# All casts of a LayerNorm on one engine, and the input loaded in eight transfers instead of two

## The chip, the cores and the metric

The kernel runs on all 8 cores of one Trainium2 chip. Each core computes one of the 8 sequences of the batch on its own; the cores exchange nothing. The metric is the device time of the slowest core in microseconds (us).

## The reference, cut to what matters

x has the shape (8, 2048, 1024): per core 2048 tokens of 1024 features. One layer is computed, a feed-forward block, an attention block with its own MLP, and the same feed-forward block again:

```python
x = x + 0.5 * ffn(layernorm(x), W_r, W_k, W_v, mu_r, mu_k)
x = x + attn(layernorm(x), ...)      # two more LayerNorms inside: ln1 ahead of the attention, ln2 ahead of the MLP
x = x + 0.5 * ffn(layernorm(x), W_r, W_k, W_v, mu_r, mu_k)

def layernorm(x, eps=1e-5):
    m = mean(x); v = var(x)
    return (x - m) / sqrt(v + eps)

def ffn(x, ...):
    x_prev = x shifted by one token
    xr = mu_r * x + (1 - mu_r) * x_prev ; xk = mu_k * x + (1 - mu_k) * x_prev
    return sigmoid(xr @ W_r.T) * (square(relu(xk @ W_k.T)) @ W_v.T)
```

The statistics of ln1 are worked out from those of the LayerNorm ahead of it, so the kernel measures mean and variance four times: ahead of the first feed-forward block, ahead of the attention, ahead of the MLP, and ahead of the second feed-forward block.

## The kernel before, in words

The data lie with features on the partitions: 8 chunks (`CH`) of 128 features, each with 2048 tokens (`T`) in its row. `S` is the f32 buffer [128, 8 x 2048] with x; chunk c stands in the columns T*c to T*(c+1). In the DRAM tensor `x_in` the layout is the same.

Work is put into one list for each engine by a small class: `p.t` is TensorE (PE), `p.v` VectorE (DVE), `p.s` ScalarE (ACT), `p.y` DMAs issued by SyncE (SP), `p.g` DMAs issued by GpSimd (POOL). An engine runs its list in order. Each operation waits for marks, pairs of a semaphore's name and a count; "T", "V" and "S" count finished operations of PE, DVE and ACT, and each DMA adds 16 to a semaphore of its own choice. `p.flush()` closes a block of the program, and at its boundary the engines wait for each other's instruction streams, though not for the DMAs issued.

**The loading.** In the first block SP issues three small loads (constants, a row of ones, ident) and then x_in in two DMAs of 4 chunks each, `DI0` and `DI1`; POOL issues one load of bconsts with a cast to bf16. `in_chunk_marks` gives for each chunk the mark that its readers wait for. In the second block POOL issues the loads of the three weights of the feed-forward block, wkT, wvT and wrT, each 4 MB of f32 in DRAM, cast on the way to 2 MB of bf16.

**The LayerNorm statistics**, `emit_ln` (line 308), work in two halves of 1024 tokens. For one half:

1. Each of the 8 chunks is cast from f32 to bf16 into a scratch buffer: ACT takes the chunks with even c (line 324), DVE those with odd c (line 330).
2. PE adds up over the 128 partitions: a matmul with a single column of ones, two per chunk (512 tokens each), 16 in all, accumulated in two PSUM tiles (line 341). A pair waits for the cast of its chunk.
3. DVE squares each chunk of the scratch in place as soon as PE has read it (line 352).
4. PE adds up the squares with 16 more matmuls (line 362). They stand behind all 16 of step 2 in PE's list.
5. When the last is done, DVE and ACT work on single rows of 512 tokens: mean, mean of squares, variance (lines 375 to 384), logarithm and exponential on ACT (387, 390), and the product (393), first for one group of 512 tokens, then the other.

The casts of the second half are written to another scratch buffer; in the lists of ACT and DVE they stand behind the row work of the first half. After both halves, `emit_outer_pair` (line 402) spreads the rows over 128 partitions with f32 matmuls of one partition, and the mixing or the application of the LayerNorm follows on DVE. `emit_ln_tiles` calls the two, from four places: lines 469 (used by both feed-forward blocks), 635 and 1090.

In the calls behind the first, the whole input of the LayerNorm is ready when the block with the casts begins. In the first call the casts wait for x_in.

Of the kernel before, what the change touches and what calls it, by code (L numbers as in the profile page):

```python
# [9 lines left out]
AF = mybir.ActivationFunctionType  # L10
# [3 lines left out]
T = 2048  # L14
CH = D // 128
# [5 lines left out]
TH = 1024  # L21
# [209 lines left out]
def build_program(host, dumps=(), stop_after=None):  # L231
    nc = bass.Bass("TRN2", target_bir_lowering=False)
    p = Prog(nc)
# [18 lines left out]
    with ExitStack() as es:  # L252
# [30 lines left out]
        W_INIT = [("DC", d_id), ("DBC", d_bc)]  # L283
# [9 lines left out]
        def emit_dump(name, buf, wait, bf16=False):  # L293
            if name not in dump_names:
                return
            if bf16:
                dm = p.g(lambda e, name=name, buf=buf: e.dma_start(dump_aps[name], buf[:, :]),
                         wait=list(wait), sem="DGD")
                gate = ("DGD", dm)
            else:  # L300
                dm = p.y(lambda e, name=name, buf=buf: e.dma_start(dump_aps[name], buf[:, :]),
                         wait=list(wait), sem="DD")
                gate = ("DD", dm)
            p.v(lambda e: e.nop(), wait=[gate])
            p.s(lambda e: e.nop(), wait=[gate])


        def emit_ln(pool, X, scratch, pre_w=(), pre_w_chunk=None, scratch2=None):
            inv_tile = [None] * NTQ
            neg_tile = [None] * NTQ  # L310
            half_T_end = [0, 0]
            scr_of = [scratch, scratch2 if scratch2 is not None else scratch]
            for half in range(2):
                scratch = scr_of[half]
                cast_marks = []
                for c in range(CH):
                    w = list(pre_w)
                    if pre_w_chunk is not None:
                        w.append(pre_w_chunk[c])
                    if half > 0 and scratch2 is None:  # L320
                        w.append(("T", half_T_end[0]))
                    if c % 2 == 0:
                        cm = ("S", p.s(lambda e, c=c, half=half, X=X, scratch=scratch:
                                       e.activation(
                            scratch[:, TH * c:TH * (c + 1)],
                            X[:, T * c + TH * half: T * c + TH * half + TH],
                            AF.Identity), wait=w, inc=True))
                    else:
                        cm = ("V", p.v(lambda e, c=c, half=half, X=X, scratch=scratch:
                                       e.tensor_copy(  # L330
                            scratch[:, TH * c:TH * (c + 1)],
                            X[:, T * c + TH * half: T * c + TH * half + TH]),
                            wait=w, inc=True))
                    cast_marks.append(cm)
                t1a, i1a, pw1a = pool.acq()
                t1b, i1b, pw1b = pool.acq()
                s1tiles = [t1a, t1b]
                c_done = []
                for c in range(CH):
                    for tt in range(2):  # L340
                        p.t(lambda e, tile=s1tiles[tt], c=c, tt=tt, scratch=scratch: e.matmul(  # L341
                            tile[0:1, :], bsl("ones", 0, 1),
                            scratch[:, TH * c + TQ * tt: TH * c + TQ * tt + TQ],
                            start=(c == 0), stop=(c == CH - 1)),
                            wait=[cast_marks[c]] +
                                 ([pw1a] if (pw1a and c == 0 and tt == 0) else []) +
                                 ([pw1b] if (pw1b and c == 0 and tt == 1) else []),
                            inc=(tt == 1))
                    c_done.append(p.c["T"])
                sq_marks = []  # L350
                for c in range(CH):
                    vm = p.v(lambda e, c=c, scratch=scratch: e.tensor_tensor(
                        scratch[:, TH * c:TH * (c + 1)], scratch[:, TH * c:TH * (c + 1)],
                        scratch[:, TH * c:TH * (c + 1)], ALU.mult),
                        wait=[("T", c_done[c])], inc=True)
                    sq_marks.append(vm)
                t2a, i2a, pw2a = pool.acq()
                t2b, i2b, pw2b = pool.acq()
                s2tiles = [t2a, t2b]
                for c in range(CH):  # L360
                    for tt in range(2):
                        p.t(lambda e, tile=s2tiles[tt], c=c, tt=tt, scratch=scratch: e.matmul(  # L362
                            tile[0:1, :], bsl("ones", 0, 1),
                            scratch[:, TH * c + TQ * tt: TH * c + TQ * tt + TQ],
                            start=(c == 0), stop=(c == CH - 1)),
                            wait=[("V", sq_marks[c])] +
                                 ([pw2a] if (pw2a and c == 0 and tt == 0) else []) +
                                 ([pw2b] if (pw2b and c == 0 and tt == 1) else []),
                            inc=(tt == 1))
                half_T_end[half] = p.c["T"]  # L370
                mm_done = ("T", p.c["T"])
                for tt in range(2):
                    j = 2 * half + tt
                    sl = slice(TQ * j, TQ * (j + 1))
                    p.v(lambda e, tile=s1tiles[tt], sl=sl: e.tensor_scalar(
                        statA[0:1, sl], tile[0:1, :], float(INVD), None, ALU.mult),
                        wait=[mm_done], inc=True)
                    p.v(lambda e, tile=s2tiles[tt], sl=sl: e.tensor_scalar(
                        bB[0:1, sl], tile[0:1, :], float(INVD), None, ALU.mult), inc=True)
                    vrel = p.c["V"]  # L380
                    p.v(lambda e, sl=sl: e.tensor_tensor(
                        bA[0:1, sl], statA[0:1, sl], statA[0:1, sl], ALU.mult),
                        wait=[("V", p.c["V"])], inc=True)
                    vv = p.v(lambda e, sl=sl: e.tensor_tensor(
                        bB[0:1, sl], bB[0:1, sl], bA[0:1, sl], ALU.subtract),
                        wait=[("V", p.c["V"])], inc=True)
                    p.s(lambda e, sl=sl: e.activation(bB[0:1, sl], bB[0:1, sl], AF.Ln,
                                                      bias=ccol(EPS)[0:1, :], scale=1.0),
                        wait=[("V", vv)], inc=True)
                    sv = p.s(lambda e, sl=sl: e.activation(bB[0:1, sl], bB[0:1, sl],  # L390
                                                           AF.Exp, scale=-0.5), inc=True)
                    inv_tile[j] = ("S", sv)
                    nm = p.v(lambda e, sl=sl: e.scalar_tensor_tensor(
                        statA[0:1, sl], statA[0:1, sl], -1.0, bB[0:1, sl],
                        ALU.mult, ALU.mult), wait=[inv_tile[j]], inc=True)
                    neg_tile[j] = ("V", nm)
                    pool.rel(i1a if tt == 0 else i1b, ("V", vrel))
                    pool.rel(i2a if tt == 0 else i2b, ("V", vrel))
            return {"inv": inv_tile[-1][1], "neg": neg_tile[-1][1],
                    "inv_tile": inv_tile, "neg_tile": neg_tile}  # L400
# [48 lines left out]
        sbS = esS.enter_context(nc.sbuf_tensor("S", [128, CH * T], F32, side="right"))  # L449
# [5 lines left out]

        sv_in = sbS[:, :].rearrange("p (c t) -> p c t", t=T)
        xv_in = x_in.rearrange("p (c t) -> p c t", t=T)
        d_in = []
        for hh in range(2):
            d_in.append(p.y(lambda e, hh=hh: e.dma_start(  # L460
                sv_in[:, 4 * hh:4 * (hh + 1), :], xv_in[:, 4 * hh:4 * (hh + 1), :]),
                sem=["DI0", "DI1"][hh]))
        in_chunk_marks = [(["DI0", "DI1"][c // 4], d_in[c // 4]) for c in range(CH)]
        emit_dump("p0", sbS, [in_chunk_marks[-1]] + W_INIT)
        p.flush()

        def emit_ffn(X, XR, XK, KA, wr, wk, wv, rt, t1f, krl, wmarks, pre_w,
# [68 lines left out]
            for q in range(4):  # L536
# [24 lines left out]
                for dv in range(CH):  # L561
# [10 lines left out]
                    for c in range(CH):  # L572
# [44 lines left out]
                        sem="DSS")  # L617
# [4 lines left out]
        if stop_after == "ffn1":  # L622
# [21 lines left out]
                         wait=[hs_marks[3]], sem="DSH")  # L644
        d_spill_h2 = p.y(lambda e: e.dma_start(spvh[:, 4:8, :], sbhv[:, 4:8, :]),
                         wait=[mark_hs], sem="DS2")
# [4 lines left out]
            wait=[("V", uq)], inc=True)  # L651
# [12 lines left out]
        if stop_after == "p2a":  # L664
# [41 lines left out]
                       wait=spill_gate, inc=True)  # L706
# [624 lines left out]
```

How the kernel before makes its waits and increments, by code:

```python
        def run(eng, fn=fn, wait=wait, incs=tuple(incs)):  # L151
            for sn, v in wait:
                eng.wait_ge(self.sems[sn], v)
            inst = fn(eng)
            for sn, amt in incs:
                inst = inst.then_inc(self.sems[sn], amt)
```

## Time and profile before

| | |
|---|---|
| median of 2 runs | 2610.68 us (2608.85 to 2612.51) |
| profiled execution | 2612.49 us |
| its slowest core, from first to last instruction | 2611.0 us (the 8 cores: 2595.4 to 2611.0) |
| instructions on that core | 26590 |
| data moved by DMA on that core | 88.11 MB |

The profile names the engines PE (TensorE), PEld (its weight loads), DVE, ACT, POOL and SP; L324 is line 324 of the kernel. A DMA queue is q0 for what POOL issues (software_dynamic) and q1 for what SP issues (hardware_dynamic); both are served by the same 16 DMA engines. A packet in these views is one row of a transfer, the contiguous piece of one partition, or the 4-byte write to the semaphore that ends an engine's part of a transfer. Sizes are those written: a weight's row of 16 KB in bf16 is read as 32 KB of f32. TensorE's clock has two levels, 1.2 and 2.4 GHz; a granted clock of 0.50 in a stretch is the lower one all through, 1.00 the upper.

### The profile page before, as it was taken

The page shows a single profiled execution, that of the slowest core. Times are in us where ns is not written, and L with a number is a line of the kernel's source. Part 1 is how long each engine was busy: PE and PEld are TensorE (multiplying, and loading weights), DVE is VectorE, ACT ScalarE, POOL GpSimd, SP SyncE. Part 2 cuts the span into 40 slices and gives each one's busy share as a digit, 9 for nine tenths or more (in the row PEclk, how much of TensorE's full clock was granted, in tenths as well). Part 3 has the DMA queues.
Part 4 walks back from the last instruction along what each step waited for, and adds up shares of the span by engine and source line. Part 5 has one row for each costly group of instructions (what it writes and reads, how often), then busy time and mean ns, then how long its engine had stood idle before and what let it go on. Part 6 is the DMA issues. An engine that isn't in the chain of part 4 may idle for free. (4 is left out here: it accounts for less than half of the span.)

```text
span 2611.0 us, 26590 instructions; the slowest of 8 cores (2595.4 to 2611.0 us)
## 1 busy us (share of the span) xinstructions
PE 1569.1 (60%) x5849; PEld 566.7 (22%) x5960; DVE 1027.2 (39%) x1688; ACT 745.0 (29%) x918; POOL 12.6 (0%) x26
## 2 busy tenths in 40 slices
PE   1446685016767778677765595266666665327665
PEld 0112231002222222222221241022222221003322
DVE  1586735763344343443432035302020000667661
ACT  0112222021544554445444312112222221202221
POOL 0000000000000000000000000000000000000000
PEclk9678896558778787777777896599999999658888
DMA  9000003302000000000021300900000001700003
GB/s 220 16 1 1 1 1 129 129 4 45 4 16 15 4 15 8 11 16 3 4 91 44 50 1 1 152 10 1 1 1 1 1 1 53 173 0 1 1 1 129
DMA packets 7739, 88.11 MB, mean 34 GB/s; under 512 B 1201, under 2 KB 3378, under 8 KB 4658
## 3 DMA queue, kind: packets, MB, share of 16 engines
q0 software_dynamic: 3168, 33.84, 7.8%
q1 hardware_dynamic: 4434, 52.56, 5.9%
q8 instruction: 72, 1.18, 0.2%
q14 instruction: 65, 0.53, 0.1%
HBM read 92.97 MB, written 25.17 MB: 45 GB/s over the span
## 5 line engine op out<-in xcount | busy, mean ns | idle before, releaser
L909 ACT ACTIVATE AT<-sd 128x1024 bf16<-128x1024 f32 x320 | 327.7, 1024 | 299.2 <-PE sd L898 282.5
L946 PE MATMUL pb<-AT,VA 128*65 128x512 bf16 x640 | 228.5, 463 | 123.1 <-DVE QB L853 47.5
L1206 PE MATMUL pq<-HMt,f2U 128*128 128x512 bf16 x503 | 155.5, 384 | 174.6 <-ACT HMt L1199 145.2
L741 PE MATMUL pb<-x,Wu 128*128 128x512 bf16 x735 | 199.4, 416 | 65.7 <-DMA Wu<-Upm 59.6
L1234 DVE SCALAR_TENSOR_TENSOR H<-pq,csts,H 128x512 f32<-128x512 f32 x32 | 24.0, 751 | 484.6 <-PE pq L1226 481.8
L1199 ACT ACTIVATE HMt<-pq,csts 128x512 bf16<-128x512 f32 x128 | 88.0, 687 | 369.8 <-PE pq L1190 369.8
L898 PE MATMUL sd<-QB,KB 64*128 64x512 bf16 x640 | 132.8, 446 | 53.3 <-ACT AT L909 51.7
L751 DVE CAST Pq<-pb 128x512 bf16<-128x512 f32 x96 | 66.4, 692 | 221.3 <-PE pb L741 218.9
L920 DVE TENSOR_TENSOR AT<-AT,bcst 128x512 bf16<-128x512 bf16 x256 | 108.9, 425 | 112.6 <-ACT AT L909 87.0
L1190 PE MATMUL pq<-P1t,f1V 128*128 128x512 bf16 x501 | 134.4, 388 | 7.8 <-ACT P1t L1172 4.0
L946 PEld LDWEIGHTS pb<-AT,VA 128*65 128x65 bf16 x640 | 69.6, 122 | 261.4 <-issue 245.2
L741 PEld LDWEIGHTS pb<-x,Wu 128*128 128x128 bf16 x768 | 80.3, 105 | 170.8 <-issue 103.2
L1206 PEld LDWEIGHTS pq<-HMt,f2U 128*128 128x128 bf16 x512 | 49.2, 96 | 304.7 <-issue 276.4
L564 PE MATMUL pq<-KA,wvS 128*128 128x512 bf16 x251 | 66.9, 410 | 56.0 <-DVE S L588 48.1
L564 PE MATMUL pp<-KA,wvS 128*128 128x512 bf16 x251 | 64.9, 401 | 58.4 <-DVE S L588 50.9
L848 DVE CAST brl<-pb 64x512 bf16<-64x512 f32 x64 | 43.7, 683 | 107.0 <-PE pb L843 103.0
L544 PE MATMUL pq<-XK,wkS 128*128 128x512 bf16 x250 | 57.7, 390 | 38.1 <-DVE bnd L484 37.9
L544 PE MATMUL pp<-XK,wkS 128*128 128x512 bf16 x250 | 57.4, 388 | 38.1 <-DVE bnd L484 37.8
L898 PEld LDWEIGHTS sd<-QB,KB 64*128 64x128 bf16 x640 | 36.8, 96 | 146.1 <-issue 138.8
L833 ACT ACTIVATE lnt<-pb 1x512 f32<-1x512 f32 x64 | 37.6, 588 | 108.0 <-PE pb L946 105.0
L573 PE MATMUL pq<-XR,wrS 128*128 128x512 bf16 x251 | 62.1, 388 | 0.3
L573 PE MATMUL pp<-XR,wrS 128*128 128x512 bf16 x251 | 61.5, 385 | 0.3
(162 smaller groups left out, 1826.2 us busy)
## 6 DMA issues: line engine op xcount, KB each, us to landing
S<-x_in SPq DMA_DIRECT2D x2, 4096.0 KB, 41.4
spill_h<-H SPq DMA_DIRECT2D x2, 4096.0 KB, 12.5
H<-spill_h SPq DMA_DIRECT2D x2, 4096.0 KB, 22.1
S<-spill_s SPq DMA_DIRECT2D x2, 4096.0 KB, 21.1
x_out<-S SPq DMA_DIRECT2D x2, 4096.0 KB, 19.0
Wu<-Upm POOLq DMA_DIRECT2D x8, 768.0 KB, 8.0
wkS<-wkT POOLq DMA_DIRECT2D x2, 2048.0 KB, 23.9
wvS<-wvT POOLq DMA_DIRECT2D x2, 2048.0 KB, 39.8
```

The lines of the kernel that those rows point to most:

```text
L544: p.t(lambda e, tile=tile, dk=dk, c=c, s0=s0: e.matmul(tile[:, :], wk[:, D * c + 128 * dk:D * c + 128 * (dk + 1)], XK[:, s0 + TQ * c:s0 + ...
L564: p.t(lambda e, tile=tileKV, dv=dv, c=c, s0=s0: e.matmul(tile[:, :], wv[:, D * c + 128 * dv:D * c + 128 * (dv + 1)], KA[:, s0 + TQ * c:s0 ...
L573: p.t(lambda e, tile=tileR, dv=dv, c=c, s0=s0: e.matmul(tile[:, :], wr[:, D * c + 128 * dv:D * c + 128 * (dv + 1)], XR[:, s0 + TQ * c:s0 + ...
L741: p.t(lambda e, tile=tile, m=m, pi=pi, tt=tt, c=c, woff=woff: e.matmul(tile[:, :], Wu[:, woff + 1024 * pi + 128 * c:woff + 1024 * pi + 128 ...
L751: vm = p.v(lambda e, tile=tile, pi=pi, tt=tt: e.tensor_copy(Pq[:, T * pi + TQ * tt:T * pi + TQ * tt + TQ], tile[:, :]), wait=[("T", tmm)], ...
L898: p.t(lambda e, s=s, u=u, i=i, r0=r0, hc=hc, j=j: e.matmul(SD[s][:, TQ * u:TQ * (u + 1)], KB[r0:r0 + 64, T * hc + 128 * i:T * hc + 128 * ( ...
L909: sm = p.s(lambda e, s=s, i0=i0, pp=pp: e.activation(ATb[:, TQ * (4 * s + 2 * pp):TQ * (4 * s + 2 * pp) + 2 * TQ], SD[s][:, :], AF.Exp, sc ...
L920: mm_ = p.v(lambda e, slot=slot, d=d: e.tensor_tensor(ATb[:, TQ * slot:TQ * slot + TQ], ATb[:, TQ * slot:TQ * slot + TQ], bsl("masks", TQ ...
L946: p.t(lambda e, i=i, h=h, tC=tC, slot=slot, is_last=is_last: e.matmul(tC[0:DH + 1, :], VA[:, VAW * i + 65 * h:VAW * i + 65 * h + 65], ATb[ ...
L1190: p.t(lambda e, tile=tile, ic=ic, pc=pc: e.matmul(tile[:, :], f1V[:, 4096 * pc + 128 * ic:4096 * pc + 128 * (ic + 1)], P1t[:, TQ * pc:TQ * ...
L1199: smg = p.s(lambda e, tile=tile, ic=ic, hslot=hslot: e.activation(HMt[:, TQ * hslot:TQ * (hslot + 1)], tile[:, :], AF.Gelu_apprx_tanh, bia ...
L1206: p.t(lambda e, tileA=tileA, ic=ic, p2=p2, hslot=hslot: e.matmul(tileA[:, :], f2U[:, 512 * ic + 128 * p2:512 * ic + 128 * (p2 + 1)], HMt[: ...
```

## The change

All eight casts of a half go to ACT, in the order of the chunks, and PE waits for ACT's marks alone. x_in is loaded with eight DMAs of one chunk (1 MB) each, all issued by SP in a row; each has a semaphore of its own, for which names that other transfers use later are taken (those keep counting from there). A chunk's readers wait for its own transfer.

```diff
-                    if c % 2 == 0:
-                        cm = ("S", p.s(lambda e, c=c, half=half, X=X, scratch=scratch:
-                                       e.activation(
-                            scratch[:, TH * c:TH * (c + 1)],
-                            X[:, T * c + TH * half: T * c + TH * half + TH],
-                            AF.Identity), wait=w, inc=True))
-                    else:
-                        cm = ("V", p.v(lambda e, c=c, half=half, X=X, scratch=scratch:
-                                       e.tensor_copy(
-                            scratch[:, TH * c:TH * (c + 1)],
-                            X[:, T * c + TH * half: T * c + TH * half + TH]),
-                            wait=w, inc=True))
+                    cm = p.s(lambda e, c=c, half=half, X=X, scratch=scratch: e.activation(
+                        scratch[:, TH * c:TH * (c + 1)],
+                        X[:, T * c + TH * half: T * c + TH * half + TH],
+                        AF.Identity), wait=w, inc=True)
                     cast_marks.append(cm)
...
-                            wait=[cast_marks[c]] +
+                            wait=[("S", cast_marks[c])] +
...
+        IN_SEMS = ["DI0", "DI1", "DCT0", "DCT1", "DO0", "DO1", "DSS", "DSH"]
         d_in = []
-        for hh in range(2):
-            d_in.append(p.y(lambda e, hh=hh: e.dma_start(
-                sv_in[:, 4 * hh:4 * (hh + 1), :], xv_in[:, 4 * hh:4 * (hh + 1), :]),
-                sem=["DI0", "DI1"][hh]))
-        in_chunk_marks = [(["DI0", "DI1"][c // 4], d_in[c // 4]) for c in range(CH)]
-        emit_dump("p0", sbS, [in_chunk_marks[-1]] + W_INIT)
+        for c in range(CH):
+            d_in.append(p.y(lambda e, c=c: e.dma_start(
+                sv_in[:, c:c + 1, :], xv_in[:, c:c + 1, :]), sem=IN_SEMS[c]))
+        in_chunk_marks = [(IN_SEMS[c], d_in[c]) for c in range(CH)]
+        emit_dump("p0", sbS, list(in_chunk_marks) + W_INIT)
```

`emit_dump` does nothing in this build.

## Rows read from the trace of the kernel before

**Rows 1.** List of cores: span and mean granted clock of the slowest.

```profile
core 4: 2611.0 us, clock 0.798
```

**Rows 2.** The page, part 1: busy time, share of the span, instructions.

```profile
PE 1569.1 (60%) x5849; PEld 566.7 (22%) x5960; DVE 1027.2 (39%) x1688; ACT 745.0 (29%) x918; POOL 12.6 (0%) x26
```

**Rows 3.** Chain that ended last, fourth LayerNorm, half 0: start, us, what.

```profile
2245.81 1.07 ACT XR L324
2247.12 5.85 PE pq L341 x16
```

**Rows 4.** Timeline, first 70 us: start, us, engine, line, operation, count, idle before.

```profile
2.28 0.91 SPq L460 DMA_DIRECT2D S<-x_in  x2
...
11.61 0.55 POOL L610 DMA_DIRECT2D wrS<-wrT  x1
...
56.88 2.20 ACT L324 ACTIVATE XR<-S 128x1024 bf16<-128x1024 f32 x2 [22.22 <-DMA S<-x_in]
...
58.09 3.57 PE L341 MATMUL pp<-XR,bcst 128*1 128x512 bf16 x8 [20.85 <-ACT XR L324]
...
66.66 0.68 DVE L375 TENSOR_SCALAR statA<-pp 1x512 f32<-1x512 f32 x1 [1.90 <-PE pp L362]
```

**Rows 5.** Lines 324, 330, 341: min/median/max ns, first and last start.

```profile
L324 ACT ACTIVATE XK<-S x8: 1056/1057/1058, 77.7 to 2271.4; 128x1024 bf16<-128x1024 f32 x8
...
L330 DVE CAST XK<-S x8: 693/693/696, 78.5 to 2271.2; 128x1024 bf16<-128x1024 f32 x8
...
L341 PE MATMUL pp<-XK,bcst x16: 376/631/631, 78.9 to 84.6; 128*1 128x512 bf16 x16
```

**Rows 6.** Timeline of the second LayerNorm, half 1.

```profile
417.92 4.50 ACT L324 ACTIVATE scr<-S 128x1024 bf16<-128x1024 f32 x4
...
418.78 3.08 DVE L330 CAST scr<-S 128x1024 bf16<-128x1024 f32 x4
419.22 6.54 PE L341 MATMUL pp<-scr,bcst 128*1 128x512 bf16 x16 [12.05 <-ACT scr L324]
421.96 6.26 DVE L352 TENSOR_TENSOR scr<-scr 128x1024 bf16<-128x1024 bf16 x8
425.62 4.39 PE L362 MATMUL pp<-scr,bcst 128*1 128x512 bf16 x16
```

**Rows 7.** Seven stretches, first ACT cast to first statistic: from:to, length, busy, PEclk.

```profile
417.92:430.18 12.26, 10.81 (x33) 2.75 (x33) 8.99 (x13) 4.22 (x4) 0.00 (x0) 0.71 0.00 0
...
1591.64:1602.89 11.25, 9.74 (x33) 2.62 (x33) 8.99 (x13) 4.23 (x4) 0.00 (x0) 0.82 0.00 0
...
sum 82.85, PE 72.52 PEld 18.79 DVE 57.51 ACT 29.58 POOL 1.17; mean PE 10.36 PEld 2.68 DVE 8.22 ACT 4.23 POOL 0.17
```

**Rows 8.** The same view, outer products (L405, L413): PE busy, granted clock.

```profile
101.80:121.50 19.70, 14.28 (x14) 3.47 (x14) 4.86 (x8) 0.00 (x0) 0.00 (x0) 0.50 0.00 0
```

**Rows 9.** Waits of SP up to 100 us: total, times, longest.

```profile
SPq L195 <- PEq L195: 6.7, 1, 6.7
```

**Rows 10.** DMA by queue, 10 to 16 us: packets, MB, share of 16 engines.

```profile
q0 software_dynamic: 2, 0.03, 3.2%
```

**Rows 11.** DMA by queue, 32 to 52 us.

```profile
q1 hardware_dynamic: 110, 3.54, 51.9%
q0 software_dynamic: 111, 1.56, 49.3%
```

**Rows 12.** DMA by queue, 4 to 7 us: bconsts (q0), ident (q1).

```profile
q0 software_dynamic: 78, 0.33, 71.8%
q1 hardware_dynamic: 81, 0.04, 7.1%
```

**Rows 13.** DMA by queue, 16 to 57 us.

```profile
q1 hardware_dynamic: 212, 5.90, 42.6%
```

**Rows 14.** DMA by queue, 58 to 70 us.

```profile
q0 software_dynamic: 140, 2.03, 100.8%
```

**Rows 15.** DMA issues up to 100 us: KB, us to landing.

```profile
wrS<-wrT POOLq DMA_DIRECT2D x1, 2048.0 KB, 61.4
```

## The prediction

> **What bounds the kernel now.** First the list of cores, to know whose clock the sum is made against: core 4 is the slowest, with a span of 2611.0 us [rows 1]; the profiled execution took 2612.49 us, 1.8 us above the median of the runs shown (2610.68). Then the busy shares: the busiest engine, PE, works 60% of the span and DVE 39% [rows 2]. No engine is full, so what counts in a stretch is which chain of waits runs through it. The diff touches two places, the loading of x_in and the casts at the head of each LayerNorm half, so I read the chain around one LayerNorm: it goes through one ACT cast (1.07 us), then straight into PE's sums over the partitions (5.85 us for the first 16 matmuls; the 16 over the squares follow in PE's own order) [rows 3]. The other casts and all squares lie beside PE. Two readings follow. One half of a LayerNorm now lasts as long as PE needs for 32 matmuls, and a cast that ends earlier gives nothing. And the first LayerNorm can't begin its last work before x_in is complete: the timeline has the two issues at 2.28 us, the casts of chunks 4 to 7 at 56.88, and the first statistic of half 0 at 66.66 [rows 4].
>
> **The change, part A: all casts on ACT.** There are 4 LayerNorms of 2 halves. Seven halves have all their input at hand when the first ACT cast starts; the eighth is half 0 of the first LayerNorm, which waits for x_in (part B). In each of the seven ACT now has 4 casts and DVE 4; the diff gives ACT 8, and DVE none. The price of a cast on ACT is 1057 ns, on DVE 693 ns [rows 5]; four on ACT take 4.50 us from first start to last end, so they start every 1.148 us [rows 6].
>
> After: the eighth cast starts 7 x 1.148 = 8.04 us after the first. Its first matmul follows 1.30 us behind the start of its cast (417.92 to 419.22 [rows 6]). So PE can start on chunk 7 at 9.34 us. By then chunks 0 to 6 are summed, because a pair of matmuls takes 0.84 us even at the slow level. What remains on PE is a tail of 18 matmuls: two for chunk 7 and all 16 for the squares, which stand behind them in PE's queue. The squares themselves are ready: DVE has nothing else now, at 6.26/8 = 0.78 us each [rows 6] they keep up with the casts.
>
> The tail's price depends on TensorE's clock. Matmuls of this form took 376 ns at the fast level (2.4 GHz) and 631 ns at the slow one (1.2 GHz) [rows 5]; back to back, 16 took 4.39 us [rows 6], which makes (4.39 - 0.376)/15 = 0.268 us from one to the next when fast, and 8 took 3.57 us when slow [rows 4], (3.57 - 0.631)/7 = 0.42. With 0.17 us to the first statistic the tail costs 17 x 0.268 + 0.376 + 0.17 = 5.10 us if fast throughout, 17 x 0.42 + 0.631 + 0.17 = 7.94 if slow throughout. How it starts: now the seven stretches, from first ACT cast to first statistic, sum to 82.85 us, from 11.25 to 12.26 for a second half [rows 7], 11.84 on average. Less 1.30, 0.17 and 0.376 that is 9.99 us for 31 steps; 11 of them must be slow (11 x 0.42 + 20 x 0.268 = 9.98), so PE runs slow for about 4.6 us after a start from idle. A tail with such a start costs 11 x 0.42 + 6 x 0.268 + 0.55 = 6.8 us. In the changed kernel PE isn't idle before the tail, it works 0.84 of every 1.15 us at the slow level. The nearest row to that is the stretch of outer products, in which PE was busy 14.28 of 19.70 us and the granted clock stayed at 0.50 all through [rows 8]: so I don't expect the fast level before the tail, but expect it sooner than from idle. I take the middle of 5.10 and 6.8, which is 5.95.
>
> A half then lasts 9.34 + 5.95 = 15.3 us; seven, 107.0, against 82.85: **+24.1 us**. With fast tails it is 7 x 14.44 = 101.1, +18.2; with starts as from idle 7 x 16.1 = 113.0, +30.1; with slow tails 7 x 17.28 = 121.0, +38.1. Below zero isn't possible: the 28 DVE casts that go away lie beside PE's sums and end before them (418.78 plus 3.08 against 425.62 [rows 6]), and the statistics behind are untouched. These stretches are followed by work that waits for them, so the 24.1 us go to the end.
>
> **Part B: eight transfers for two.** x_in goes to the chip in the same bytes, now as 8 KB rows (2048 values of 4 bytes) for each partition in place of 32 KB (four chunks), 1024 rows for 256. The issues: 0.91 us for two on SP [rows 4], so eight take 3.6 us, to 5.9 us. Behind them in SP's queue is only the boundary of the block, where SP waits 6.7 us for others today [rows 9]; this is cover for the added 2.7 us. Without it, the weights would start that much later.
>
> What matters is the company. From about 16 us the weights on the software queue run beside x_in (until then that queue has 2 packets [rows 10]), and all 16 DMA engines are full. The views of the transfers by queue give the rule by which they share. From 32 to 52 us the hardware queue (x_in) moved 110 packets and the software queue (weights) 111, with 51.9% and 49.3% of the time [rows 11]: turns one for one, each turn a row, of 32 KB for either. Is it equal time or equal turns? From 4 to 7 us small rows of ident ran beside bconsts: 81 packets against 78, but with 7.1% of the time against 71.8% [rows 12]. So it is turns, whatever a row's size.
>
> The Trainium skill (DMA: Bandwidth & Descriptors, Queues, rings and completion order) says the same of turns, but that one lasts a whole packet of about 9 to 17 descriptors; by that an engine could take several 8 KB rows in a turn and x_in would keep its share. The rows above show one row in a turn.
>
> With turns of one row each: from 16 us on, 5.90 MB of x_in are left [rows 13], 180 rows of 32 KB, after the change 720 of 8 KB. The weights have 3 x 128 = 384 rows, at 1.56 us (alone they filled the engines with 100.8% of 12 us x 16 for 2.03 MB, 124 rows of 16 KB as written: 193.5/124 [rows 14]). A row of x_in costs 51.9% of 320 us over 108 rows of 3.54 MB, 1.54 us [rows 11]; a quarter is 0.39, and the 8.5 KB reads of bconsts bear it out: 71.8% of 48 us over 78 is 0.44 [rows 12]. I take 0.41. While the weights last, x_in moves 384 of its rows: 384 x (1.56 + 0.41)/16 = 47.3 us, to 63.3. The other 336 then go alone: 8.6 us, to 71.9. Today the last weights, issued at 11.61 us [rows 4], land 61.4 us later, at 73.0 [rows 15], and the bytes are the same, so the whole can't end much earlier. I take 72.5 for chunk 7, against 56.88: +15.6. The weights finish sooner, which nobody feels: their first matmul comes behind the whole LayerNorm and the first mixing. If the share is kept, this term is 0.
>
> Behind the landing something is gained. Now it takes 66.66 - 56.88 = 9.78 us to the first statistic, with 24 matmuls [rows 4]. After, only chunk 7 is left: 1.30 us to its matmul and 6.8 for a tail from near idle, 8.1. So -1.7. Part B: **+13.9 us**.
>
> Sum: 24.1 + 13.9 = +38.0 us on 2612.49 = 2650.5; on the median, 2648.7.
>
> **Rivals.**
> - *x_in keeps its share.* The engine takes several small rows in a turn, chunk 7 lands near 56.9. For it stands only that no row shows 8 KB beside 32 KB reads; the ident rows speak against it [rows 12]. It gives -1.7 + 24.1 = +22.4, 2633 us. The page's packet of many descriptors, named above, would have this result.
> - *The tail never gets the fast level.* PE's work in pairs with gaps lasts 9 us a half, and the row of the outer products shows a slow stretch at 72% busy [rows 8]; against it, the unbroken tail is like today's starts, all of which rose. 13.9 + 38.1 = +52, 2663 us.
> - *Faster.* The small rows get ahead of the weights altogether. Alone, 256 rows at 1.54 us on 16 engines take 24.6 us, from about 8 us on: landing at 33, 24 us earlier than now. It decides when the landing is earlier than part A costs: even with fast tails, 18.2 - 1.7 = 16.5 us, before 40.4 us. Then the time is 2610.7 - 24 + 16.5 = 2603. One for one in every stretch speaks against it.
>
> **How the numbers follow.** Forecast 0.66, with its own range from fast tails (13.9 + 18.2, 2643) to tails as from idle (13.9 + 30.1, 2655); share kept 0.22 (2627 to 2639 with the same two tails); slow tails 0.10; faster 0.02. The range of 8 in 10 goes from 2629, which leaves out the low end of the second case, to 2660. By 2%, about what a measurement of this kernel can tell from no change, the borders are 2558.5 and 2662.9: only the third case reaches the upper one, and about half of it passes. Faster 0.01, same 0.93, slower 0.06.
>
> **What would show it.** In the changed profile: eight L324 casts in a row, 1.148 us apart, and no DVE cast; seven stretches of about 15.3 us; one for one in the packets by queue, with x_in at about a fifth of the time between 20 and 60 us; the cast of chunk 7 at 72 to 73 us, chunks 2 and 3 at 26 and 42; the weights' last landing near 64; the first statistic near 80.6. The forecast is wrong if chunk 7 lands under 65 us, if the tails last under 5 us or near 8, or if a later stage, which sees only shifted starts, changes its length.

## The result

The changed kernel took 2652.5 us in the median of 11 runs (2643.2 to 2668.5), the kernel before 2609.5 us (10 runs, 2607.3 to 2612.6). The ratio is 1.017, with a 95% interval from 1.0142 to 1.0199: slower, by 37 to 52 us. The forecast was 2649 us, +38.0, with a range from 2629 to 2660, and 0.93 for a change within 2%.

The profiled execution took 2647.3 us; its slowest core is again core 4, with 2645.7 us against 2611.0 [rows 1], +34.7. The mean over the eight cores went from 2603.1 to 2637.7, +34.7 as well. (Five of the eleven runs, those from 2657 us up, had the cores of one die or of both at a granted clock of 0.776 to 0.794, mostly below 0.79, instead of about 0.797, and the other six have a median of 2645.0 us, 35.6 above the kernel before; executions that a lower clock made clearly longer, here one of 3471 us, are left out, here and in the experiments.)

The first 80 us of core 4 after the change, which answer to [rows 4]: start, us, engine, line, operation, count, and the idle time before with what ended it (`...` marks lines left out, here and below). Line 322 is now the cast on ACT, 333 and 354 are PE's two sums, 367 is the first statistic.

```profile
2.27 5.11 SPq L453 DMA_DIRECT2D S<-x_in  x8
...
34.21 1.06 ACT L322 ACTIVATE XR<-S 128x1024 bf16<-128x1024 f32 x1 [14.15 <-DMA S<-x_in]
...
49.79 1.06 ACT L322 ACTIVATE XR<-S 128x1024 bf16<-128x1024 f32 x1 [14.52 <-DMA S<-x_in]
...
70.62 1.06 ACT L322 ACTIVATE XR<-S 128x1024 bf16<-128x1024 f32 x1 [1.66 <-DMA S<-x_in]
71.82 1.01 PE L333 MATMUL pp<-XR,bcst 128*1 128x512 bf16 x2 [1.71 <-ACT XR L322]
72.62 5.34 PE L354 MATMUL pp<-XR,bcst 128*1 128x512 bf16 x16
...
78.14 0.68 DVE L367 TENSOR_SCALAR statA<-pp 1x512 f32<-1x512 f32 x1 [4.44 <-PE pp L354]
```

The cast of the last chunk starts at 70.6 us instead of 56.9, and each cast before it waited for its transfer. The first statistic comes at 78.1 instead of 66.7, 11.5 us later. The queues from 20 to 45 us (packets, MB written, share of the 16 engines) show why, beside [rows 11]:

```profile
q0 software_dynamic: 225, 3.41, 78.1%
q1 hardware_dynamic: 229, 1.66, 21.7%
```

229 packets of x_in against 225 of weights, one for one as before, but a fifth of the time for x_in, where it had half. Equal counts alone would also come of longer turns with equal numbers of rows. The times of the single packets in the same trace settle it: from 20 to 60 us, 293 of the 336 rows of weights begin within 5 ns of the end of a row of x_in, and 27 within 5 ns of the end of another row of weights. So on each engine a row of weights follows a row of x_in, and with equal counts that makes turns of a single row.

And the weights were through early: the third landed 51.0 us after its issue at 10.98, at 62.0, against 73.0 before [rows 15].

```profile
wrS<-wrT POOLq DMA_DIRECT2D x1, 2048.0 KB, 51.0
```

The other part of the time, in the second LayerNorm, half 1, beside [rows 6]:

```profile
434.24 9.10 ACT L322 ACTIVATE scr<-S 128x1024 bf16<-128x1024 f32 x8
435.54 8.95 PE L333 MATMUL pp<-scr,bcst 128*1 128x512 bf16 x16 [12.05 <-ACT scr L322]
...
444.28 5.44 PE L354 MATMUL pp<-scr,bcst 128*1 128x512 bf16 x16
...
449.90 0.68 DVE L367 TENSOR_SCALAR statA<-pp 1x512 f32<-1x512 f32 x1 [4.54 <-PE pp L354]
```

ACT's eight casts take 9.1 us, PE's first sum stretches from 6.5 to 8.95 us because it waits for them, and the 16 matmuls over the squares follow only then: 15.66 us where it was 12.26. The seven stretches of [rows 7], as stretches of the changed kernel (length, then the busy times, and PEclk in the third place from the end):

```profile
88.71:102.94 14.23, 11.13 (x33) 2.59 (x33) 6.22 (x9) 8.45 (x8) 0.00 (x0) 0.76 0.01 2
...
434.24:449.90 15.66, 13.36 (x33) 2.67 (x33) 6.22 (x10) 8.45 (x8) 0.00 (x0) 0.59 0.00 1
...
sum 105.72, PE 88.72 PEld 18.24 DVE 41.48 ACT 59.16 POOL 0.60; mean PE 12.67 PEld 2.61 DVE 5.93 ACT 8.45 POOL 0.09
```

105.72 - 82.85 = 22.9 us. With the 11.5 us of the first half that makes 34.4 of the 34.7 us by which core 4 grew; all other stages together moved by 0.3 us.

### The profile page after: what moved, and what is told of

Its sections match the earlier page's. It is cut to its first block and busy times, and to the rows that moved or that the text cites. A ratio compares the mean times of both kernels' runs of the same rounds, so it can differ in the third digit from the quotient of the medians.

```text
span 2645.7 us, 26598 instructions; the slowest of 8 cores (2624.9 to 2645.7 us)
## 1 busy us (share of the span) xinstructions
PE 1589.3 (60%) x5849; PEld 566.7 (21%) x5960; DVE 1005.0 (38%) x1656; ACT 778.8 (29%) x950; POOL 12.0 (0%) x26
## 5 line engine op out<-in xcount | busy, mean ns | idle before, releaser
L733 PE MATMUL pb<-x,Wu 128*128 128x512 bf16 x735 | 201.3, 419 | 65.3 <-DMA Wu<-Upm 59.2
L556 PE MATMUL pq<-KA,wvS 128*128 128x512 bf16 x251 | 66.7, 409 | 57.7 <-DVE S L580 49.7
```

The source lines that it names most:

```text
L556: p.t(lambda e, tile=tileKV, dv=dv, c=c, s0=s0: e.matmul(tile[:, :], wv[:, D * c + 128 * dv:D * c + 128 * (dv + 1)], KA[:, s0 + TQ * c:s0 ...
L733: p.t(lambda e, tile=tile, m=m, pi=pi, tt=tt, c=c, woff=woff: e.matmul(tile[:, :], Wu[:, woff + 1024 * pi + 128 * c:woff + 1024 * pi + 128 ...
```

## The experiments

Ratios are against the kernel before, run on the same chip, with 95% intervals; they compare means. The medians of the kernel before, from which the differences below are taken, were 2610.9 us beside the first four runs of the table, 2611.3 beside the next three and merged, and 2610.9 beside x_four and merged2. "Seven stretches" and "first statistic" are means over the eight cores, read from their timelines; before the change they are 82.2 us and 64.6 us, with the changed kernel 104.0 us and 78.9 us. An empty field was not read.

| kernel | median us | ratio | first statistic | seven stretches |
|---|---|---|---|---|
| casts alone (a_casts) | 2632.9 | 1.0084 (1.0067 to 1.0100) | 65.3 | 104.0 |
| transfers alone (b_transfers) | 2625.1 | 1.0050 (1.0032 to 1.0069) | 79.5 | 82.5 |
| both (after_again) | 2646.8 | 1.0137 (1.0115 to 1.0159) | 79.0 | 104.0 |
| transfers, small rows of weights (w_split) | 2599.5 | 0.9954 (0.9937 to 0.9971) | 54.0 | 82.5 |
| casts, other order on PE (a_casts_inter) | 2616.8 | 1.0026 (1.0016 to 1.0035) | 63.2 | 89.8 |
| eight transfers, weights held (w_held) | 2588.5 | 0.9926 (0.9901 to 0.9950) | 42.4 | |
| two transfers, weights held (w_held2) | 2589.8 | 0.9929 (0.9910 to 0.9948) | 44.2 | |
| four transfers (x_four) | 2629.6 | 1.0070 (1.0045 to 1.0094) | 79.9 | 82.7 |
| both halves under the transfers (merged) | 2577.5 | 0.9872 (0.9856 to 0.9889) | 41.9 | |
| the same, other order on DVE (merged2) | 2573.9 | 0.9857 (0.9837 to 0.9876) | 39.8 | |

**The casts alone.** The changed kernel with the two old transfers; the cut is against the changed kernel.

```diff
-        for c in range(CH):
-            d_in.append(p.y(lambda e, c=c: e.dma_start(
-                sv_in[:, c:c + 1, :], xv_in[:, c:c + 1, :]), sem=IN_SEMS[c]))
+        for hh in range(2):
+            d_in.append(p.y(lambda e, hh=hh: e.dma_start(
+                sv_in[:, 4 * hh:4 * (hh + 1), :], xv_in[:, 4 * hh:4 * (hh + 1), :]),
+                sem=["DI0", "DI1"][hh]))
...
```

> Part A of the change alone: all casts on ACT, x_in still in two transfers. My theory (two costs that add up): chunks 4 to 7 land as before, near 57 us; ACT's four casts and the tail of 18 matmuls behind them put the first statistic of the first half at 67 to 68 us (66.7 on core 4 before), and the seven other stretches from first ACT cast to first statistic sum to about 104 to 107 us against 82 to 83. Time +22 to +26 us, 2632 to 2636 us, ratio 1.009. Rival 1 (the casts alone cost all of the change): ratio 1.017. Rival 2 (scatter of the changed kernel, whose runs lay between 2643 and 2668 us, comes with the ACT casts): the runs of this kernel scatter over 20 us too.

+22.1 us. The seven stretches are at 104.0 us as in the changed kernel, 21.8 longer than before, the first statistic only 0.7 us later. The five runs lay between 2631.4 and 2635.2 us, so no scatter of 20 us comes with the ACT casts.

**The transfers alone.** The kernel before with the eight transfers.

```diff
-        for hh in range(2):
...
+        for c in range(CH):
+            d_in.append(p.y(lambda e, c=c: e.dma_start(
+                sv_in[:, c:c + 1, :], xv_in[:, c:c + 1, :]), sem=IN_SEMS[c]))
...
```

> Part B alone: x_in in eight transfers, casts split between ACT and DVE as before. My theory: each DMA engine takes one row from each queue in turn, so the 8 KB rows of x_in get a fifth of the time beside the weights; chunk 7 lands at 70 to 73 us. DVE squares everything only after its own cast of chunk 7, so the tail behind the landing is about 8 to 9 us and the first statistic is at 79 to 81 us, 13 to 15 us later than before. The seven other stretches are unchanged at 82 to 83 us. Time +13 to +15 us, 2623 us, ratio 1.005. Rival (the transfers cost nothing, all is in the casts): ratio 1.000, landing at 57. Rival 2 (the scatter comes with the transfers): runs scatter over 20 us.

+14.2 us, with the first statistic 14.9 us later and the stretches untouched (82.5 us against 82.2); its five runs lay within 2.0 us. Its timeline behind the last landing:

```profile
71.64 0.69 DVE L330 CAST XR<-S 128x1024 bf16<-128x1024 f32 x1 [5.62 <-DMA S<-x_in]
72.44 6.26 DVE L352 TENSOR_TENSOR XR<-XR 128x1024 bf16<-128x1024 bf16 x8
...
79.66 0.68 DVE L375 TENSOR_SCALAR statA<-pp 1x512 f32<-1x512 f32 x1 [0.96 <-PE pp L362]
```

All eight squares stand behind DVE's own cast of chunk 7, though seven of the chunks had been there for long. So it took 8.0 us from the cast, in the mean of the cores too, where the changed kernel needed 7.7 in the mean (7.5 on its slowest core); 0.3 us is all that ACT's casts give back in that place.

**Both again.**

> The changed kernel once more, beside its two parts on one chip. If the two parts simply add: a_casts plus b_transfers, +35 to +40 us. The sum of the stages in the profiles was +34 to +36 us, while the timed median was +43 with a wide scatter (2643 to 2668 us). If the scatter belongs to the kernel, it is there again; if it belonged to that chip, the runs lie within a few us of 2645.

+36.0 us, and the two parts add up to 22.1 + 14.2 = 36.3. No interplay shows. The three runs lay from 2646.0 to 2648.9: the wide scatter of the first measurement did not come back on this chip. The two ratios, 1.017 and 1.0137, have intervals that overlap.

**Smaller rows for the company.** This tells turns from bytes: x_in keeps its 8 KB rows, and only the rows beside it shrink.

```diff
-        dwk = p.g(lambda e: e.dma_start(wkS[:, :], dram["wkT"]), sem="DWK")
+        for k in range(CH):
+            dwk = p.g(lambda e, k=k: e.dma_start(wkS[:, D * k:D * (k + 1)],
+                                                 dram["wkT"][:, D * k:D * (k + 1)]), sem="DWK")
...
```

> As b_transfers, but each of the three weights is loaded in 8 pieces of 1024 columns, so that its rows are read as 4 KB (written as 2 KB) instead of 32 KB. Same bytes. One row of each queue in turn (mine): a row of weights now costs about 0.2 us of an engine beside 0.41 for a row of x_in, x_in gets two thirds of the time; 720 rows left at about 16 us x 0.61/16 = 27 us, chunk 7 lands at 43 to 46 us, the first statistic at 52 to 55 us, some 12 us before the kernel before and 26 before b_transfers; time about 2597 us, ratio 0.995. Rival (equal bytes or equal time for the queues): landing near 57 us or later, as the number of rows would not matter. Rival 2 (the number of transfers of x_in is what slows it, not their rows beside the weights' rows): landing stays at 70 us or more.

The same bytes, and the sign turned: chunk 7's cast started at 46.0 us in the mean, the first statistic came 25.5 us earlier than with whole rows of weights, the time fell by 26 us below b_transfers and 11 below the kernel before. The queues from 20 to 45 us:

```profile
q1 hardware_dynamic: 696, 4.99, 59.2%
q0 software_dynamic: 864, 1.58, 43.2%
```

x_in has 59% of the time instead of 22%. The packets include the completions, of which the weights in 24 pieces have many more; without them it is 532 rows of weights against 529 of x_in from 20 to 40 us. Both rivals fall: it is not equal bytes or time, and not the number of transfers of x_in, which is still eight.

**Another order on PE.** All casts on ACT, two transfers; only PE's list changes. `sum2(c)` issues the two matmuls over the squares of chunk c, inside the loop that issues the sum over each chunk.

```diff
-                for c in range(CH):
-                    vm = p.v(lambda e, c=c, scratch=scratch: e.tensor_tensor(
...
+                    sq_marks.append(p.v(lambda e, c=c, scratch=scratch: e.tensor_tensor(
...
+                    if c > 0:
+                        sum2(c - 1)
+                sum2(CH - 1)
```

> As a_casts (all casts on ACT, two transfers), but in PE's order the sum over the squares of chunk c-1 stands right behind the sum of chunk c, for all eight halves. My theory: ACT's eight casts cost so much only because all 16 matmuls over the squares stand behind the last of them; with the new order at most 4 to 6 matmuls are left behind the last cast, so a half ends 11.5 to 12.5 us after its first cast, the sum of the seven is 81 to 88 us against 104 in a_casts and 82 before. The first half of the first LayerNorm gains too, since only chunks 6 and 7 are left behind the fourth cast: about 4 us. Time within 5 us of the kernel before, 2607 to 2614 us, ratio 0.998 to 1.001. Rival (the ACT casts themselves, or DVE and ACT getting in each other's way, cost the time): ratio stays near 1.008.

+5.5 us: 16.6 us of the 22.1 came back, and with them the rival falls that the ACT casts themselves cost the time. The seven stretches fell from 104.0 to 89.8 us, a bit more than the 88 I had as the upper end; the time is 3 us above the 2614 I had, and the first statistic came 2.0 us earlier than in a_casts, not about 4. ACT is still eight casts long (DVE and ACT work as in a_casts), so most of what the casts cost came of what stood behind the last of them. The stretch of core 5 in half 1 of the second LayerNorm:

```profile
415.68:428.46 12.78, 10.73 (x33) 2.64 (x33) 6.22 (x9) 8.45 (x8) 0.00 (x0) 0.76 0.00 1
```

12.78 us, against 9.1 for the casts alone: what is left behind them is two sums, a square between them, and the waits from engine to engine. Against the kernel before the stretches are still 7.6 us longer, and the first statistic is 1.3 us earlier, where the squares of the early chunks no longer wait; together 6.3 us, about the 5.5 that are missing. I put most of the 7.6 us down to ACT's pace for eight casts, which was not tested by itself. It is not all of it: in the stretch shown the last cast ends at 424.8 us and PE begins the sum of its chunk at 426.0, behind the square sums ahead of it in its list.

**The weights held back.** In w_held eight transfers, in w_held2 two; in both POOL issues the weights only when x_in is complete. The diff is the same single wait:

```diff
-        dwk = p.g(lambda e: e.dma_start(wkS[:, :], dram["wkT"]), sem="DWK")
+        dwk = p.g(lambda e: e.dma_start(wkS[:, :], dram["wkT"]), wait=list(in_chunk_marks), sem="DWK")
```

> As b_transfers (eight transfers, casts split), but the loads of the three weights wait for all of x_in. My theory (the rows of x_in are slow only for their company): x_in alone fills the engines, 256 x 32 KB at 1.54 us on 16 engines from about 8 us, chunk 7 lands at 33 to 35 us; first statistic at 42 to 44 us, 22 us before the kernel before; the weights land by about 75 us and hold nobody up. Time 2587 to 2590 us, ratio 0.991 to 0.992. Rival (eight transfers of 8 KB rows are slow by themselves): chunk 7 lands at 50 us or later.

> The kernel before (two transfers, casts split) with the weights' loads behind x_in. It tells whether eight transfers bring anything once the company is gone. Mine: x_in complete at 33 to 35 us in this one too, then 9 to 10 us to the first statistic, so within 2 us of w_held, ratio 0.991 to 0.993. Rival (8 KB rows move slower or faster than 32 KB rows even alone): a difference of over 3 us between the two.

Both came as expected: 0.9926 and 0.9929. Eight transfers bring 1.7 us at the first statistic (42.4 against 44.2), 1.3 us in the time, no difference that these intervals can tell. Chunk 7's cast in w_held, and the weights that follow at once:

```profile
34.77 0.69 DVE L330 CAST XR<-S 128x1024 bf16<-128x1024 f32 x1 [5.16 <-DMA S<-x_in]
35.14 0.53 POOL L608 DMA_DIRECT2D wkS<-wkT  x1 [32.92 <-DMA S<-x_in]
```

So 8 KB rows are not slow by themselves. The transfer that mattered was made to wait by one that nobody needed yet.

**Four transfers.** Rows of 16 KB, nothing else changed.

```diff
+        for k in range(4):
+            d_in.append(p.y(lambda e, k=k: e.dma_start(
+                sv_in[:, 2 * k:2 * (k + 1), :], xv_in[:, 2 * k:2 * (k + 1), :]),
+                sem=["DI0", "DI1", "DO0", "DO1"][k]))
...
```

> The kernel before with x_in in four transfers of two chunks, rows of 16 KB. One row of each queue in turn: from about 16 us 360 rows are left at 0.77 to 0.8 us, beside 384 rows of weights at 1.56: 360 x 2.35/16 = 53 us, chunk 7 lands at 68 to 70 us (56.9 with 32 KB rows on core 4, 71 to 73 with 8 KB), the first statistic at 77 to 79 us, time +12 us, ratio 1.004 to 1.005. Rival (each added transfer costs a fixed 2.5 us, 15 us for six): two added transfers put the landing at 61 to 62 us, ratio 1.002.

The packets from 20 to 45 us are one for one again, with a third of the time for x_in:

```profile
q0 software_dynamic: 191, 2.87, 66.8%
q1 hardware_dynamic: 191, 2.87, 34.1%
```

The last ACT cast started at 71.4 us in the mean, not at 68 to 70, as late as with eight transfers: with 16 KB rows x_in has 360 rows left at 16 us by the sum above and the weights 384, so both end nearly together. The third weight landed 61.0 us after its issue, where it was 61.4 in the kernel before. Rows of 8 KB, then, delay the end of x_in no further. A fixed price per transfer falls: it would have put the landing at 61 to 62. The time was +18.7 us, 6.7 more than I expected and nominally 4.4 more than with eight. The first statistic (+0.4) and the stretches (+0.2) don't explain that. In the mean of the cores the two kernels still start the second LayerNorm together (409.9 and 409.8 us) and the third 2.1 us apart (1583.3 and 1581.2), so about half of the difference comes from the attention block, which the edit does not touch. The intervals of the two ratios overlap, and the rest stays open.

**A version that beats both.** In merged, with eight transfers and held weights, the first LayerNorm works on both halves of a chunk as it lands: ACT casts the one, DVE the other, PE sums both and then the squares of the chunk before.

```diff
+            for c in range(CH):
+                w = list(pre_w) + [pre_w_chunk[c]]
+                cm0 = ("S", p.s(lambda e, c=c: e.activation(
...
+                cm1 = ("V", p.v(lambda e, c=c: e.tensor_copy(
...
+                pair(s1, c, 1, cm1)
+                pair(s1, c, 0, cm0)
...
+                if c > 0:
+                    for half in (1, 0):
+                        pair(s2, c - 1, half, sq_marks[c - 1, half])
```

> A version meant to beat both kernels: w_held, and the first LayerNorm works on both halves as each chunk lands (ACT casts the one half, DVE the other, PE sums both, the sums over the squares of chunk c-1 behind them). All but chunk 7 lies under the transfers. Expected: chunk 7 lands at 33 to 35 us, the first statistic at 38 to 40 us, and the second half's 11.7 us of casts and sums are gone. Against w_held: 3 to 5 us at the first statistic and 11 to 12 us for the second half, so about -15 us, 2572 to 2576 us, ratio 0.985 to 0.987. Rival (PE at the slow clock can't keep up with a chunk each 3.1 us, 8 matmuls of 0.42 us being 3.4): the backlog shifts the first statistic to 42 us or later, and the gain against w_held is 11 us or less.

0.9872, -33.7 us, and at 2577.5 us just outside the 2572 to 2576 expected. The second half's casts and sums are gone from the chain, but the first statistic was at 41.9 us in the mean, not 38 to 40, and the gain on w_held was 10.9 us. Those are the numbers of the rival, a PE that can't keep up. The timeline shows another cause:

```profile
34.87 1.06 ACT L425 ACTIVATE XR<-S 128x1024 bf16<-128x1024 f32 x1 [1.89 <-DMA S<-x_in]
...
36.54 0.69 DVE L436 TENSOR_TENSOR XK<-XK 128x1024 bf16<-128x1024 bf16 x1 [0.94 <-PE pp L415]
...
38.13 0.69 DVE L428 CAST XK<-S 128x1024 bf16<-128x1024 f32 x1
...
42.39 0.68 DVE L450 TENSOR_SCALAR statA<-pp 1x512 f32<-1x512 f32 x1 [1.15 <-PE pp L415]
```

ACT casts chunk 7 at 34.9 us, DVE only at 38.1. DVE's cast stands behind the squares of the chunk before, and the first of these waits 0.94 us for PE, which itself had waited 1.03 us for DVE's cast of that same chunk (its two matmuls start at 35.74 us). So DVE needs 3.22 us for a chunk (from its cast at 34.91 us to that at 38.13), while the chunks land 2.95 us apart (ACT's casts at 31.92 and 34.87), and falls behind. In merged2 DVE's cast of chunk c+1 stands ahead of the squares of chunk c (the cut is against merged).

```diff
                 pair(s1, c, 0, cm0)
...
+                if c > 0:
+                    squares(c - 1)
+                if c + 1 < CH:
+                    casts(c + 1)
```

> As merged, with DVE's list put in another order: the cast of chunk c+1 no longer stands behind the squares of chunk c, which wait for PE and ACT. In merged DVE fell a chunk behind (its cast of chunk 7 started at 38.1 us, ACT's at 34.9) and the first statistic came at 42.4 us. Expected: DVE's cast of chunk 7 at 35 us, first statistic at 40 to 41 us, about 2 us less than merged, 2575 us, ratio 0.986. Rival (the lag came from the landing or from PE's clock): first statistic stays at 42 us or later.

```profile
35.23 1.06 ACT L427 ACTIVATE XR<-S 128x1024 bf16<-128x1024 f32 x1 [3.09 <-DMA S<-x_in]
35.26 0.69 DVE L430 CAST XK<-S 128x1024 bf16<-128x1024 f32 x1 [1.86 <-DMA S<-x_in]
...
40.06 0.68 DVE L466 TENSOR_SCALAR statA<-pp 1x512 f32<-1x512 f32 x1 [0.93 <-PE pp L415]
```

Both casts at 35.2 us, the first statistic 2.1 us earlier in the mean of the cores with the same work on PE, so it was the order on DVE: 2573.9 us, a ratio of 0.9857, 37 us less than the kernel before.

## Why the prediction was right, point by point

**The forecast.** +38.0 us; measured +43 (37 to 52) at first, +36.0 on the second chip, +34.7 on core 4 between the two profiled executions. The likeliest case was the one that happened, with both of its terms. The stages that were forecast give less than the first +43: over the cores part A measured +21.8 and the first statistic +14.3 (from 64.6 to 78.9 us), 36.1 in all, where the mean span grew by 34.7.

**Part A, the casts.** Predicted +24.1 us, from seven stretches of 15.3 us; measured +22.9 on core 4, +21.8 over the cores (104.0/7 = 14.9 us each), and +22.1 for the casts alone. The pace of 1.148 us held (9.10 us for eight). The tail was 14.9 - 9.34 = 5.5 us against 5.95. The step on the clock, no fast level before the tail, held only in part. On core 4 it held in six of seven stretches, where the granted clock averages 0.58 to 0.65; in the seventh (88.71 to 102.94 us) it averages 0.76. Over all cores there are 56 stretches. In 33 the clock was 0.50 from 1.3 to 9.3 us behind the first cast, so all through the paired matmuls, and they last 15.26 us in the mean (14.67 to 15.92), the 15.3 of the forecast. In the other 23 it had risen before the tail, and they last 14.27 us (14.23 to 14.31), near the 14.4 of the case with fast tails. So +24.1 us was too high because two stretches in five were of the other kind, and not because a tail was sized wrongly. Why the clock rose in one stretch and not in the next, no run here shows.

**Part B, the transfers.** Predicted: chunk 7 at 72.5 us, +15.6; measured 70.6 on core 4, +13.7, and over the cores 71.2 against 55.2 before, +16.0 (core 4 had been the last of all before). The rule of turns was right: the counts by queue in the changed kernel, in w_split and in x_four go one for one or nearly so, and the times of the packets show turns of a single row, of 8, 16 or 32 KB. With longer turns for the short rows, equal in bytes, x_in would by the prediction's sum have kept its landing near 57 us. The Trainium skill (DMA: Bandwidth & Descriptors, Queues, rings and completion order) has turns too, but of a whole packet, typically about 9 to 17 descriptors. The trace does not agree: 293 of 336 rows of weights follow a row of x_in directly. What I mis-sized is small: a row of weights beside the 8 KB rows, at 78.1% of 400 us over about 208 rows of 3.41 MB, cost 1.50 us, not 1.56. The intermediate landings I had wrong by 8 us (chunks 2 and 3 at 34 and 50 us, not 26 and 42). About 3 us of it is the start: 6.12 MB of x_in were left at 16 us, not the 5.90 MB taken from the kernel before. For the rest, the sum went by the mean of 16 engines, and a chunk lands with its slowest; the likely cause, which was not tested.

**Behind the landing.** Predicted -1.7 us (8.1 from the cast to the first statistic); measured 78.14 - 70.62 = 7.5 on core 4, so -2.3; over the cores 7.7 against 9.4 before, -1.7. b_transfers shows that most of this would have come without the casts on ACT (8.0 us).

**The cover.** SP took 5.11 us for its eight issues, to 7.4 us, more than the 3.6 I added up from two (4.8 to 6.8 us over the cores); the weights were issued no later than before (9.94 us for the first). The cover held.

**The rivals.** "x_in keeps its share" falls with the packets by queue and with w_split. "The tail never gets the fast level" falls with the stretch lengths: the longest of the 56 is 15.9 us, against 17.3. "Faster" needed the landing before 40 us, which only holding the weights brought.

**The size of a turn** was worth its chance as a rival: the whole of part B hung on it, and two rows of small transfers at the start of the trace [rows 12] decided it rightly. They showed equal counts for unequal rows, which rules out turns of equal bytes; that a turn is one row was read into them, and only the times of the packets show it.

## What to carry to other kernels

When two queues share the DMA engines, look at the size of the rows in each: cutting an urgent transfer into pieces with shorter rows takes bandwidth from it and gives it to whatever runs beside it with longer rows. First ask whether the other transfer is needed yet; one wait (-21.5 us in w_held2) brought more than cutting the weights' rows (-11.4 in w_split). And work that is moved to another engine is paid for by what stands in order behind its last piece: let the dependent work follow each piece, before you count the pieces.

## What the runs showed of the hardware that I had not expected

- Two queues share the engines by rows over a wide span: 229 to 225 with rows of 8 KB beside 32 KB reads, 191 to 191 with 16 KB, and 110 to 111 with 32 KB [rows 11]; the share of time followed the rows' length (22%, 34%, 52%). From 20 to 60 us in the changed kernel 293 of 336 rows of weights begin within 5 ns of the end of a row of x_in; for the small rows of bconsts beside ident, before the change, it is 75 of 77 from 4.5 to 7 us.
- SP needed 5.11 us for eight issues of 1 MB in a row (0.64 us each), against 0.91 for two (0.46 each), and 6.16 us in w_held (slowest core of each).
- While PE worked in pairs of matmuls with gaps, one pair every 1.15 us for 9 us, the granted clock stayed at its lower level in 33 of 56 stretches of the changed kernel and rose to the upper in 23; the ones that rose were 1.0 us shorter in the mean (14.27 against 15.26 us).
